# GpSimd sums the scan terms of the first batch, weights rounded on ScalarE and clipped on VectorE, sums of squares of the keys as rows

## What is computed

```
x += tanh(g0) * mamba(ctx, z = layernorm(x))      # state-space scan over 512 steps, 16 states, 512 channels
x += tanh(g1) * bitffn(layernorm(x))              # weights rounded to -1, 0, 1; rows rounded to 8 bits
x += tanh(g2) * attention(layernorm(x), ctx)      # 16 heads of 128, q and k normalised by their mean square
x += tanh(g3) * experts(layernorm(x))             # token i goes to expert i % 4

mamba:   state[n] = exp(delta * A[n]) * state[n] + delta * u * B[n];   y = sum over n of state[n] * C[n] + D * u
weights: w_dq = clip(round(w / gamma), -1, 1) * gamma,  gamma = mean(|w|)
keys:    k = (ctx @ Wk) per head, divided by sqrt(mean(k^2) + eps)
```

## Time and profile before

| | us |
|---|---|
| median of 3 runs | 2017.95 |
| lowest and highest | 2015.21, 2027.63 |
| time of the profiled execution | 2014.32 |
| its span, first to last instruction | 2012.5 |
| TensorE busy | 1856.5 (92%) |
| VectorE busy | 1386.6 (69%) |
| ScalarE busy | 936.6 (47%) |
| GpSimd busy | 616.6 (31%) |

### The profile page before, as it was taken

One profiled execution on the slowest core, in us unless ns is written; L12 is line 12 of the kernel. 1 busy time (PEld: TensorE's weight loads), 2 busy tenths in 40 slices (PEclk: granted clock), 3 DMA queues, 4 the chain that ended last, 5 costly groups with the idle time before them and its releaser, 6 DMA issues.

```text
span 2012.5 us, 20103 instructions
## 1 busy us (share of the span) xinstructions
PE 1856.5 (92%) x6442; PEld 884.7 (44%) x6442; DVE 1386.6 (69%) x2076; ACT 936.6 (47%) x1848; POOL 616.6 (31%) x621
## 2 busy tenths in 40 slices
PE   7799998977998799999978999999998989999999
PEld 3355453433444234544433454444444434444543
DVE  4789876899996869988865999896764354431321
ACT  5856565544754355654624555654433333330100
POOL 1133321123644114454610335554312342320100
PEclk8789988988999889999988999999999999999999
DMA  6699952176775003887810257884101399874210
GB/s 236 210 265 284 275 181 101 53 202 154 195 194 140 12 22 94 206 207 186 205 56 18 58 152 180 243 199 117 43 21 59 112 277 272 254 208 183 94 52 32
DMA packets 159463, 304.40 MB, mean 151 GB/s; under 512 B 13944, under 2 KB 46968, under 8 KB 156416
## 3 DMA queue, kind: packets, MB, share of 16 engines
q1 hardware_dynamic: 140928, 236.01, 37.5%
q0 software_dynamic: 18432, 67.12, 17.2%
HBM read 177.64 MB, written 58.33 MB: 117 GB/s over the span
## 4 chain that ended last, share of the span: by engine, by line
PE 72%; DVE 11%; ACT 5%; issue 4%; DMA 4%; POOL 2%; SPq 1%; DVEq 0%; ACTq 0%; POOLq 0%
PE p L757 9%; PE p L710 8%; PE p L747 8%; PE p L727 8%; PE p L684 6%; PE p L794 6%; PE p L679 4%; PE p L600 4%; PE p L733 4%; PE p L691 3%; PE p L809 3%; PE p L645 2%; DMA s_U<-in_Wq 2%; PE p L581 1%; DVE s_U L1057 1%
## 5 line engine op out<-in xcount | busy, mean ns | idle before, releaser
L927 DVE TENSOR_TENSOR_SCAN s_M<-s_M 128x1024 f32<-128x1024 f32 x128 | 302.9, 2367 | 18.2 <-ACT s_M L1164 15.7
L1057 DVE CUSTOM_DVE_ANT_0 s_U<-p,s_U 128x512 f32<-128x512 f32 x256 | 187.3, 744 | 171.5 <-PE p L727 169.1
L727 PE MATMUL p<-s_U 128*128 128x512 f32 x512 | 269.3, 613 | 1.8 <-DMA s_U<-k_scratch 1.2
L710 PE MATMUL p<-s_U 128*128 128x512 f32 x512 | 254.7, 604 | 12.7 <-DMA s_U<-in_Wq 11.0
L1383 POOL DMA_DIRECT2D s_u<-s_M x128 | 113.5, 887 | 436.4 <-DVE s_M L932 395.7
L1427 POOL TENSOR_SCALAR s_U<-s_U 128x512 f32<-128x512 f32 x256 | 227.7, 913 | 5.9
L757 PE MATMUL p<-s_U 128*128 128x512 f32 x512 | 223.6, 592 | 0.0
L747 PE MATMUL p<-s_U 128*128 128x512 f32 x472 | 212.9, 594 | 2.4 <-DMA s_U<-p_scratch 1.6
L1294 ACT ACTIVATE s_U<-s_U 128x512 f32<-128x512 f32 x256 | 181.8, 719 | 57.4 <-DVE s_U L1061 57.4
L1299 ACT COPY s_U<-p 128x512 f32<-128x512 f32 x196 | 107.0, 591 | 173.8 <-PE p L733 170.3
L1164 ACT ACTIVATE s_M<-s_dl,s_small 128x511 f32<-128x511 f32 x256 | 170.3, 717 | 33.0 <-DVE s_M L927 32.8
(11 more groups left out here) (178 smaller groups left out, 2509.4 us busy)
## 6 DMA issues: line engine op xcount, KB each, us to landing
s_u<-s_M POOLq DMA_DIRECT2D x128, 512.0 KB, 7.3
s_bc<-bc_scratch SPq DMA_DIRECT2D x128, 256.0 KB, 4.9
k_scratch<-s_U SPq DMA_DIRECT2D x16, 1024.0 KB, 7.4
v_scratch<-s_U SPq DMA_DIRECT2D x16, 1024.0 KB, 6.3
s_U<-in_Wq SPq DMA_DIRECT2D x64, 256.0 KB, 7.8
s_U<-k_scratch SPq DMA_DIRECT2D x64, 256.0 KB, 5.0
s_U<-in_Wo SPq DMA_DIRECT2D x64, 256.0 KB, 4.3
s_U<-rk_scratch SPq DMA_DIRECT2D x64, 256.0 KB, 5.2
```

The source lines that it names most:

```text
L710: ins = e.matmul(banks[bk][:], wqq[j % 2][:, k, :], axT[b % 2][:, k, :], start=(k == 0), stop=(k == 3))
L727: e.matmul(banks[bk][:], qT[j % 3][:, k * 128:(k + 1) * 128], kT[j % 2], start=True, stop=True).then_inc(S["a_s"], 1)
L927: e.tensor_tensor_scan(w, dA[i % 2], w, 0.0, ALU.mult, ALU.add).then_inc(S["m_s"], 1)
L1057: e.tensor_tensor_reduce(out=Pm[j % 2][:, k, :], in0=banks[ABANK[kind, j, k]][:], in1=rkb[j % 2], scale=rq[:, k:k + 1], scalar=-3.0e38, op ...
```

## The change

1. In batch 0 alone, GpSimd adds each term to `u` with an instruction of its own, in place of the accumulating DMA. Batches 1 to 3 keep the DMA. The products D*u move behind the first scan, and the zero columns of the two exp buffers are set halfway through and at the end of `soft`.
2. Rounding the weights: ScalarE scales and adds the rounding constant (`rnd`), VectorE clips in one instruction (`clip`), ScalarE subtracts the constant (`put`). The next block's load is issued by ScalarE behind `put` instead of by SyncE. On VectorE the planner now puts Q ahead of M.
3. Sums of squares of the keys: four matmuls with the ones as weights, one for each head, with 512 moving columns. The result is 128x512, each group of 32 partitions holding copies of one head's row. ScalarE scales all of it, four small DMAs spread the four rows over 128x16, GpSimd raises that to the power, and one DMA writes it to DRAM, for each of the 16 pairs.
4. F: the transposes of the rounded row go before the scale's parts are written (`f_q`, then `f_z` for the fifth one). The largest absolute value is taken over each 512 behind each `m` part and once over four numbers. The last rounding step over 2048 is in two halves, each with its own signal.
5. Attention's scores wait for the square of the queries (`a_qs`), which follows the copy that they waited for before. Some planner durations change with all this.

```diff
-                        e.dma_start(u[:, 2 * g:2 * g + 2, :], two(wy[s]), accum_op=ALU.add).then_inc(S[f"d_w{s}"], 16)
+                        y = u[:, 2 * g:2 * g + 2, :]
+                        if b:
+                            e.dma_start(y, two(wy[s]), accum_op=ALU.add).then_inc(S[f"d_w{s}"], 16)
+                        else:
+                            e.tensor_tensor(y, y, two(wy[s]), ALU.add).then_inc(S["m_ad"], 1)
...
                         e.tensor_tensor_scan(w, dA[i % 2], w, 0.0, ALU.mult, ALU.add).then_inc(S["m_s"], 1)
+                        if i == 0:
+                            e.wait_ge(S["m_h0"], 2 * b + 2)
+                            for t in range(4):
+                                e.tensor_scalar(u[:, t, :], u[:, t, :], Dv[:, t:t + 1], None, ALU.mult).then_inc(*v.up())
...
-                        e.tensor_scalar(src, src, thr[:, w:w + 1], 1.0, ALU.mult, ALU.min).then_inc(*v.up())
-                        e.wait_ge(*v.now())
-                        e.tensor_scalar(src, src, -1.0, MAGIC, ALU.max, ALU.add).then_inc(S["q_rnd"], 1)
+                    elif kind == "clip":
+                        e.wait_ge(S["q_rnd"], 4 * w + c + 1)
+                        e.tensor_scalar(stg[c], stg[c], MAGIC - 1.0, MAGIC + 1.0, ALU.max, ALU.min).then_inc(S["q_cut"], 1)
...
+                    elif kind == "rnd":
+                        e.activation(stg[c], stg[c], ACT.Copy, bias=MAGIC, scale=thr[:, w:w + 1]).then_inc(S["q_rnd"], 1)
                     elif kind == "put":
-                        e.wait_ge(S["q_rnd"], i + 1)
+                        e.wait_ge(S["q_cut"], i + 1)
                         e.activation(dst, stg[c], ACT.Copy, bias=-MAGIC, saturate=False).then_inc(S["q_put"], 1)
+                        if w < 2:
+                            e.wait_ge(S["q_put"], i + 1)
+                            load_stage(e, w + 1, c)
...
-FIRST = {"PE": "MFAQKE", "DVE": "AFMQKE", "ACT": "AFMQKE", "POOL": "MAFQKE", "DMA": "QMAFKE", "SUM": "MAFQKE"}
+FIRST = {"PE": "MFAQKE", "DVE": "AFQMKE", "ACT": "AFMQKE", "POOL": "MAFQKE", "DMA": "QMAFKE", "SUM": "MAFQKE"}
...
                         for h in range(4):
-                            for t in range(4):
-                                ins = e.matmul(banks[bk][:, 4 * h + t:4 * h + t + 1], ksq[h][:, t * 128:(t + 1) * 128], ones[:, 0:1], start=True, stop=True)
+                            ins = e.matmul(banks[bk][32 * h:32 * h + 32, :], ones[:], ksq[h], start=True, stop=True)
...
-                        e.activation(krs[:, 16 * b:16 * b + 16], banks[bk][:, 0:16], ACT.Copy, bias=EPS, scale=1.0 / HD).then_inc(S["k_nv"], 1)
+                        if n:
+                            e.wait_ge(S["d_ksr"], 64 * n)
+                        e.activation(ksr, banks[bk][:], ACT.Copy, bias=EPS, scale=1.0 / HD).then_inc(S["k_nv"], 1)
...
+                    if kind == "pw":
+                        n = NB * q + b
+                        power(krs[:, 16 * n:16 * n + 16], (S["d_ksr"], 64 * (n + 1)), "k_p")
...
                     elif kind == "r":
+                        e.wait_ge(S["k_nv"], n + 1)
+                        for h in range(4):
+                            e.dma_start(krs[32 * h:32 * h + 32, 16 * n:16 * n + 16],
+                                        ksr[32 * h:32 * h + 1, :].rearrange("o (p c) -> o p c", c=16)).then_inc(S["d_ksr"], 16)
+                    elif kind == "st":
+                        e.wait_ge(S["k_p"], n + 1)
+                        e.dma_start(rkd[j:j + 4].rearrange("h (p c) -> (h p) c", c=16), krs[:, 16 * n:16 * n + 16]).then_inc(S["d_rk"], 16)
...
                         e.scalar_tensor_tensor(h[:, ch * 512:(ch + 1) * 512], banks[LBANK[b, "v", t, ch]][:], qt[:, 13:14], ti, ALU.mult, ALU.mult).then_inc(S["f_h"], 1)
+                        e.wait_ge(S["f_h"], i + 1)
+                        e.tensor_reduce(qt[:, 24 + ch:25 + ch], h[:, ch * 512:(ch + 1) * 512], AXX, ALU.max, apply_absolute_value=True).then_inc(*v.up())
                     elif kind == "l" and k == 0:
-                        e.wait_ge(S["f_h"], 4 * f + 4)
-                        e.tensor_reduce(qt[:, 16:17], h, AXX, ALU.max, apply_absolute_value=True).then_inc(*v.up())
+                        e.wait_ge(*v.now())
+                        e.tensor_reduce(qt[:, 16:17], qt[:, 24:28], AXX, ALU.max).then_inc(*v.up())
```

More of the change, by code:

```diff
@@ L59 @@
 for w in range(3):
-    QUANT += [("abs", w, c) for c in range(4)] + [("put", w, c) for c in range(4)]
+    QUANT += [("abs", w, c) for c in range(4)] + [("thr", w, 0)]
+    for c in range(5):
+        QUANT += [("rnd", w, c)] if c < 4 else []
+        QUANT += [("put", w, c - 1)] if c else []
+        QUANT += [("clip", w, c)] if c < 4 else []
     if w == 1:
@@ L64 @@
 MAMBA = [("conv", t) for t in range(4)] + [("silu", 0), ("xp", 0), ("dt", 0), ("exp", 0), ("one", 0)]
-MAMBA += [("soft", i) for i in range(8)] + [("init", 0)]
+MAMBA += [("soft", i) for i in range(4)] + [("init", 0)] + [("soft", i) for i in range(4, 8)]
 MAMBA += [(k, i) for i in range(2 * NS) for k in ("mul", "scan", "out")]
@@ L114 @@
     for b in range(NB):
-        KV += [(b, q, "k", i) for i in range(4)] + [(b, q, "v", 0)] + ([(NB - 1, q - 1, "r", 0)] if q and b == 0 else [])
-        KV += [(b, q, "v", 1), (b, q, "n", 0), (b, q, "v", 2), (b, q, "nv", 0), (b, q, "v", 3)]
-KV += [(NB - 1, 3, "r", 0)]
+        last = ((b - 1) % NB, q - (b == 0))
+        KV += [(b, q, "k", i) for i in range(4)] + [(b, q, "v", 0), (b, q, "v", 1), (b, q, "n", 0), (b, q, "v", 2), (b, q, "nv", 0)]
+        KV += [(*last, "pw", 0)] if q or b else []
+        KV += [(b, q, "v", 3), (b, q, "r", 0)] + ([(*last, "st", 0)] if q or b else [])
+KV += [(NB - 1, 3, "pw", 0), (NB - 1, 3, "st", 0)]
 KBANK = {}
 for x in KV:
-    if x[2] != "nv":
+    if x[2] in "kvn":
         KBANK[x] = len(KBANK) % 3
@@ L229, in forward @@
             if k % 2:
-                part(name, [("DVE", 1.6)], ("m", t, k - 1), free=pair)
+                part(name, [("DVE", 2.3)], ("m", t, k - 1), free=pair)
             else:
@@ L242, in forward @@
         elif k == 0:
-            part(name, [("DVE", 5.4)], ("m", t, 7))
+            part(name, [("DVE", 3.6)], ("m", t, 7))
         elif k < 3:
@@ L376, in plan @@
             done[name] = ended[s, i, k]
-        if k == max(n for n, (on, _) in enumerate(does) if on not in ("POOL", "DMA") or len(does) == 1):
+        if k == max((n for n, (on, _) in enumerate(does) if on not in ("POOL", "DMA")), default=0):
             for x in gives:
@@ L540, in pe_quant @@
                 for kind, w, c in QUANT:
-                    if kind == "put" and c == 0:
+                    if kind == "thr":
                         e.wait_ge(S["p_set"], 8)
@@ L663, in pe_keys @@
                 for b, q, kind, i in KV:
-                    if kind == "nv":
+                    if kind not in "kvn":
                         yield
@@ L961, in quant_row @@
                 e.wait_ge(*v.now())
-                e.tensor_scalar(dst, src, MAGIC, 127.0, ALU.subtract, ALU.min).then_inc(*(last or v.up()))
+                n = src.shape[1] // len(done)
+                for i, up in enumerate(done):
+                    e.tensor_scalar(dst[:, n * i:n * i + n], src[:, n * i:n * i + n], MAGIC, 127.0, ALU.subtract, ALU.min).then_inc(*up)
             def dve_ffn(b):
@@ L1508, in sp_quant @@
                 for kind, w, c in QUANT:
-                    if kind == "abs" and (w or c >= 2):
-                        load_stage(w, c)
+                    if kind == "abs" and w == 0 and c >= 2:
+                        load_stage(e, w, c)
                     if (kind, w, c) == QUANT[-1]:
```

162 lines of the change are left out of this document (73 added, 89 removed).

## The result

| | before | after |
|---|---|---|
| median | 2016.68 us (2015.21 to 2027.63, 4 runs) | 2051.38 us (2047.54 to 2052.87, 4 runs) |
| profiled execution, its span | 2014.32, 2012.5 | 2050.62, 2048.8 |
| ratio | | 1.0157, 95% interval 1.0118 to 1.0196 |

The change makes the kernel 1.6% slower. The forecast was 2033 in 1968 to 2068. The stages of the changed kernel, in the columns of the earlier trace rows: preparation, the scan loop of batch 0, the rest of M, F of batch 0, then M of batch 1 beside attention, its tail behind the last scan, and F of batch 1.

What follows compares the result with a forecast made beforehand. TensorE and VectorE were both taken as near their limit. F of batch 0 starts 32 us later but shortens to 135, leaving attention's start unchanged; leftover VectorE work adds 15: 2014.3 + 15 = 2029, median 2033 us, range 1968 to 2068.

Steps and rivals of the forecast that it cites:

- Exclusion: Batch 0's scan loop: GpSimd's additions and VectorE's two-SBUF-input instructions take turns, holding VectorE 2.2 us in each step.
- the term of 70 us: Batch 0's scan loop: 32 additions holding VectorE 2.2 us each lengthen it by 70 us, at most 82.
- Rival (b): Batch 0's scan loop: GpSimd's additions run beside VectorE, the loop ends at 250, total 1968 us; chance 0.13.
- Length of the loop: Batch 0's scan loop: 151 + 70 + 10 + 8 us from a start at 81, ending at 320 instead of 254.
- n: Keys' sums of squares on TensorE: 1.1 us a pair instead of 3.5, 38 us less work over 16 pairs.
- The longer loop takes in nearly all pairs of keys, F keeps one or two: Batch 0: the longer scan loop absorbs nearly all key pairs, leaving F of batch 0 one or two instead of four.
- the 135 us of F of batch 0: F of batch 0 shortens from 167 to 135 us (bounds 120 and 155), so attention opens at 472 as before.
- Rounding at nothing: Weight rounding: ScalarE's twelve more passes of 1.91 us cost nothing, covered by VectorE's longer step in the loop.
- M of batch 1: Beside F of batch 0: 143 us of VectorE work, 122 fit, 21 left over at 472, 15 counted for the end.
- F's part "nothing": F of the later batches: 2 us each gained from a shorter chain, as much lost in VectorE work, net nothing.
- rival (a): F of batch 0 isn't shortened and lasts 155 us, so exclusion costs in full, about 2055 us; chance 0.20.
- (c): F of batch 0 takes 115 us with TensorE relieved, attention opens at 452, total about 1993 us; chance 0.23.

Runs made afterwards that it cites:

- told: Changed kernel with only the planner told that `out` takes VectorE 3.35 us in batch 0, not 1.3, so the order differs; 2047.0 us, 1.0114 to the kernel before.
- keep_dma: Changed kernel with batch 0's additions given back to the accumulating DMAs; 2015.5 us, ratio 0.9958 to the kernel before.
- round_alone: Kernel before with only the rounding part, including Q ahead of M on VectorE; 2045.5 us, ratio 1.0110.
- after: The changed kernel with all parts, against the kernel before; median 2051.38 us, ratio 1.0157.
- spare_reads: Kernel before plus, in each step of batch 0, a spare GpSimd 128x1024 addition over scratch columns nobody reads; 2080.9 us, ratio 1.0296.
- keys_order: Kernel before with only the keys' part, the planner told the old key costs so VectorE's order stays nearly as before; 2000.5 us, ratio 0.9887.
- ffn_alone: Kernel before with only F's part of the change; 2019.9 us, ratio 0.9987.
- dve_adds: Changed kernel with VectorE instead of GpSimd doing batch 0's 32 additions; 2019.5 us, ratio 0.9978 to the kernel before.
- spare_writes: Kernel before plus, in each step of batch 0, a spare GpSimd memset of 128x2048 scratch columns, which only writes; 2023.9 us, ratio 1.0003.

## Why the prediction was right, and where it was wrong

- **Exclusion: right.** Forecast 2.2 us held in each step and steps of 6.9 to 7.3 us; found 2.03 and 6.75. Only 28 of the 32 additions held an instruction, so the term of 70 us measured 57. Rival (b), that the additions run beside VectorE, is out by these rows and by the two spare kernels.
- **Length of the loop: right. Its start: wrong.** 239 us forecast, 235.8 found: the hold took 13 us less than its term, the rest more. I kept the start at 81; it was 65.6. Of these 15 us the rounding alone shows some 6 (first scan at 78.3 against 84.8), the other parts alone none; the rest appears only with the parts together, and I haven't traced it further. Behind the loop 19 us instead of 17. So F begins at 320.7, not at 337.
- **`n`: right.** 1.1 us a pair, as taken. The old form cost 4.0 us a pair on average and not the 3.5 of the row that I read, so 45 us of TensorE's work are gone instead of 38.
- **"The longer loop takes in nearly all pairs of keys, F keeps one or two": the step that failed.** Each engine goes strictly through its written order, so a loop that lasts longer takes in hardly any more parts. The changed kernel's order has 9.5 pairs ahead of the loop's end, and six are left for F of batch 0, one more than before (five, where I had read four). With it fell the 135 us of F of batch 0, which took 162.8 to attention's first matmul. `told`, with two pairs left, still takes 153 over the same stretch. So the term was wrong by some 18 us even without the keys, where waits for VectorE's rounding stood, and by some 10 for the keys. The F start that I had put 16 us too late hid half of this: attention opens at 483.5, 11.5 late.
- **Rounding at nothing: wrong.** The step said that the cover for ScalarE's passes is VectorE's longer step. It is, for the exps, which nobody waits for in the loop. But the same queue holds the copies of keys, and TensorE waits 66 us for them there, where it had no such wait; `keep_dma` has 61 such us in a loop of 195. These waits are not what left the keys over: `told` has 57 us of them and twelve pairs in its loop. The rounding reached the keys through the planner: with its passes and the new priority, the order of `round_alone` has 8.9 pairs ahead of the loop's end instead of 10.75, and seven are left.
- **M of batch 1: the size was met by luck, the discount was wrong.** I forecast 21 us left over, for an F of 135 us. F took 28 us longer, which by the same reckoning (90% of 163 us are 147) would have left nothing. Yet the last scan of batch 1 comes 26.6 us later than before; when attention opened eight of its scans had started, ten before. I counted 15 for the end. But in `after` F of batch 1 begins 37 us later, as 10 more are lost between the last scan and F, where the order has two more of attention's score parts, and the end is 36 later. `spare_reads` (57 us at F, 57 at the last batch's first query) and `keys_order` (16 us at F of batch 1, 15 there) show that with an order unchanged, or nearly, a delay or a gain of this stage reaches the end nearly whole.
- **F's part "nothing": wrong with the order held.** There 2.6 us of VectorE's work cost some 2.5 us in each of the first three F, and 0.7% in all. With its own order (`ffn_alone`) no cost was measured.
- **Total.** 2029 forecast against the profiled 2014.3, found 2050.6: +36 us where I had +15. It fell inside the range only because the range took in rival (a), to whose band (2045 to 2075) I gave 0.20; it is outside the forecast's own 2010 to 2045. It lies close to (a)'s 2055, and (a)'s condition held (F of batch 0 over 145 us). Its mechanism held only in part: with few keys F takes 146 to 148 us to its end, and what made it 159 were keys on TensorE.
- **Slips in the sums.** By my own rule the chance of faster than 1998 is 0.13 + 0.23/2 = 0.245 and not 0.27, and of slower than 2038 0.20 + 0.11 = 0.31 and not 0.32. Rival (a) starts from the profiled 2014, (b) and (c) from the median 2018.

What stays open: why `dve_adds`, with F of batch 0 25 us later than `keep_dma`, ends only 2.6 later (4 by the medians). Its gap between the last scan of batch 1 and F is 33 us instead of 43. The written orders of both have the same five score parts in that gap, and `keep_dma` two more parts of attention's output sums, so the order explains it at most in part, and I have no run that fixes it in these two.

## What to carry to other kernels

Before giving a second engine elementwise work, ask which instructions of the first will run beside it; here an addition on GpSimd, which reads SBUF, stopped two-input VectorE work for 2.03 us, 28 times in 32 steps, and the same work on VectorE or by DMA was some 2% faster. Where an order is written out in advance from a cost table, judge an edit with the order held fixed first: the same instructions gave +0.8% and -1.1%, and the parts didn't add up. For the same reason don't count on a stage that gets longer to take in more work: read from the written order what lies in it. When passes move to an engine with slack, look in its queue for everything that another engine waits for, not only for what the moved passes used to wait for.

## What the runs showed of the hardware

I hadn't expected the hold to be so clean. GpSimd's 128x1024 addition held a scan for 2.03 us in a step where it had started under the instruction before, and took 3.27 us itself; in `told` one that started at 253.83, while VectorE stood idle, took 2.34. So GpSimd waits for a running two-input instruction of VectorE, and the next one of VectorE waits for GpSimd. In `spare_reads` the scans got 2.2 us longer beside the addition alone and 3.4 where GpSimd's power over 128x16 ran too; that power took 5.1 us on average in the loop, against 3.5 in `spare_writes`. The memset over twice as many columns took 2.15 us and disturbed nothing.
